# Keys and values of one pair of batches projected among the other pair's recurrences, and half of the routing in the last attention steps

## What is computed

```python
# conditioning: forward and backward recurrences of exp(k) and exp(k)*v, k = v = fside
num = nf + nb - ekv + euk * vf
den = df + db - ek + euk
x0  = sigmoid(r) * (num / maximum(den, 1e-8)) * (0.8 + 0.2 * tf)
# attention on the conditioned rows, 16 query heads, 4 key/value heads, head size 128
h = rmsnorm(x0, ln_w)
q, k, v = h @ wq, h @ wk, h @ wv ;  q, k = apply_rope(q), apply_rope(k)
attn = softmax(causal(q @ k.T / sqrt(128)))
x1 = (attn @ v) @ wo + x0
# routing: best 2 of 8 experts of every token
h2 = rmsnorm(x1, ff_ln_w);  logits = h2 @ gate_w;  top_k(logits, 2)
```

## Time and profile before

| | us |
|---|---|
| median of 3 runs (625.84 to 627.07) | 626.72 |
| the profiled execution | 625.02 |
| its span, first to last instruction | 623.2 |
| recurrences, to the last x0 | 0 to 73 |
| last batch's hidden rows and keep-clock | 73 to 81 |
| keys and values | 81 to 108 |
| attention, steps 0 to 37 | 108 to 300 |
| routing and ranking | 300 to 328 |
| experts and second layer | 328 to 623 |

### The profile page before, as it was taken

The page is one execution under the profiler, slowest core; times in us unless marked ns, Lnnn a source line. Parts: engine busy times, 40 slices in busy tenths (PEclk is TensorE's granted clock), DMA queues, the critical chain, the costliest instruction groups (busy, mean ns, idle before and its releaser), DMA issues.

```text
span 623.2 us, 10889 instructions
## 1 busy us (share of the span) xinstructions
PE 495.9 (80%) x3862; PEld 406.4 (65%) x3862; DVE 506.2 (81%) x981; ACT 361.1 (58%) x762; POOL 241.2 (39%) x204
## 2 busy tenths in 40 slices
PE   2011298599999999999748999999999999475774
PEld 1000143278888878888618999999999999332542
DVE  4999878688888888987354979989999899489993
ACT  3336235777787778876307457565555556356671
POOL 3244014744444445541436079642514420170011
PEclk9999999989999999999859999999999999888897
DMA  8300004050000000000149799889888753130001
GB/s 267 135 1 1 0 1 135 0 178 2 1 2 2 1 2 9 19 9 2 58 157 357 259 331 281 273 267 257 300 290 271 274 130 119 34 103 17 9 25 36
DMA packets 36530, 71.87 MB, mean 115 GB/s; under 512 B 5275, under 2 KB 21915, under 8 KB 36219
## 3 DMA queue, kind: packets, MB, share of 16 engines
q10 hardware_dynamic: 15280, 40.77, 19.6%
q1 hardware_dynamic: 18123, 22.26, 10.6%
q0 software_dynamic: 3072, 8.14, 5.2%
HBM read 66.03 MB, written 5.12 MB: 114 GB/s over the span
## 4 chain that ended last, share of the span: by engine, by line
PE 55%; DVE 27%; issue 7%; ACT 5%; DMA 3%; POOL 1%; SPq 1%; DVEq 0%; ACTq 0%; POOLq 0%; PEldq 0%
PE pw L437 9%; PE pb L437 9%; PE pt L631 6%; PE pb L631 6%; PE sc L478 6%; PE sc L631 6%; PE po L437 5%; PE pt L489 3%; DVE areg L1181 2%; DVE areg L1167 2%; DVE areg L1165 2%; DVE rs L1579 2%; DMA wreg<-in_L_ffn_w 1%; DVE breg L1238 1%; DVE areg L1614 1%
## 5 line engine op out<-in xcount | busy, mean ns | idle before, releaser
L1730 POOL TENSOR_TENSOR breg<-breg,con 128x512 f32<-128x512 f32 x32 | 40.7, 1272 | 81.4 <-ACT breg L864 81.4
L437 PE MATMUL pb<-areg,wreg 128*128 128x512 f16 x240 | 58.4, 379 | 2.1 <-ACT breg L864 1.9
L437 PE MATMUL pw<-areg 128*128 128x256 f16 x406 | 56.5, 273 | 2.7 <-DVE areg L1533 2.7
L872 ACT ACTIVATE breg<-breg,mx 128x128 f32<-128x128 f32 (+1 forms) x128 | 56.5, 444 | 2.0 <-DVE mx L1289 2.0
L478 PE MATMUL sc<-areg,breg 128*128 128x128 f32 (+1 forms) x256 | 48.6, 334 | 6.7 <-DVE mx L1289 5.5
L631 PE MATMUL pb<-areg,wreg 128*128 128x128 f32 x448 | 52.7, 275 | 0.6 <-ACT areg L965 0.6
L985 ACT CAST areg<-areg 128x512 f16<-128x512 f32 (+1 forms) x46 | 25.9, 563 | 46.8 <-DVE areg L1519 43.6
L631 PEld LDWEIGHTS pb<-areg,wreg 128*128 128x128 f32 x448 | 51.3, 192 | 0.9 <-issue 0.8
L631 PE MATMUL pt<-areg,wreg 128*128 128x128 f32 x424 | 49.9, 275 | 1.3 <-DMA wreg<-in_L_ffn_w 1.3
L631 PEld LDWEIGHTS pt<-areg,wreg 128*128 128x128 f32 x424 | 48.5, 192 | 1.5 <-DMA wreg<-in_L_ffn_w 1.4
L631 PE MATMUL sc<-areg,wreg 128*128 128x128 f32 x416 | 48.9, 275 | 0.0
(11 more groups left out here) (250 smaller groups left out, 1286.4 us busy)
## 6 DMA issues: line engine op xcount, KB each, us to landing
wreg<-in_L_ffn_w ACTq DMA_DIRECT2D x40, 896.0 KB, 8.1
wreg<-in_L_ffn_w SPq DMA_DIRECT2D x14, 896.0 KB, 8.3
ys_dram<-areg ACTq DMA_DIRECT2D x23, 128.0 KB
wreg<-in_L_ffn_wq SPq DMA_DIRECT2D x1, 2048.0 KB, 8.9
wreg<-in_L_ffn_wo SPq DMA_DIRECT2D x1, 2048.0 KB, 8.2
areg<-in_fside_BxSxS ACTq DMA_DIRECT2D x4, 256.0 KB, 5.4
x_in<-in_x SPq DMA_DIRECT2D x4, 256.0 KB, 3.9
h_dram<-areg SPq DMA_DIRECT2D x8, 128.0 KB, 1.7
```

What stands on the lines that cost most here:

```text
L437: last = nc.tensor.matmul(bank, w(a), m(b), start=first and k == 0, stop=final and k == 2)
L872: last = nc.scalar.activation(pr[:, parity, b, o:o + w], pr[:, parity, b, o:o + w], ACT.Exp, bias=mx[:, parity, k:k + 1], scale=-1.0, accu ...
L1730: G.tensor_tensor(t2[:, parity, :].rearrange("p (b n) -> p b n", b=2), t2[:, parity, :].rearrange("p (b n) -> p b n", b=2), rope_sin.rearr ...
```

## The change

Instructions are moved, hardly any are added. Six edits:

1. The recurrence loop on VectorE is unrolled. Batches 0 and 1 run as before. Then scans of batch 2, the low parts of the key and value weights, the low hidden rows of batches 0 and 1, and from there the `rope` products, sine products and low value parts of n = 0 to 3 stand between the parts of batches 2 and 3. ScalarE, GpSimd and TensorE follow the same order; TensorE's keep-clock stands after batch 1.
2. ScalarE splits the key and value weights after batch 0 and the query weights after batch 1 (`qkvhi_done` counts to 2). VectorE makes the low query parts at the end of batch 3.
3. n = 4 to 7 (pair 1) are projected in steps 1 to 4, in bank pb[1], with the sine product on GpSimd. `query_place` and `key_place` give the order of all 40 rotations: keys 0 to 3, queries 0 and 1, then key, query in turn. All queries use pb[0]. The low hidden rows of batches 2 and 3 are made in step 0.
4. The output weights are split in steps 5, 7, 9 and 11.
5. Four row tiles are transposed in steps 34 to 37 and three multiplied in 35 to 37; logits go to bank sc2; 10 keep-clock products stand ahead of tile 4 and 8 behind tile 7. Keep-clock of steps 1, 2 moves to 0, 1.
6. xn, the sigmoids and the squares' waste output live elsewhere, so that nothing overlaps.

```diff
+OUT_WEIGHTS_AT = (5, 7, 9, 11)
+        def query_place(u):
+            return KVH + u + max(0, u - 1) if u <= KVH else KU + u
+        def key_place(n):
+            return n if n < KVH else KVH + 2 + 2 * (n - KVH)
+        def route_bank(i):
+            return pb[i % 2] if i >= NT // 2 else pb[0]
...
-            for b in range(B):
+            for b in range(2):
                 ratio_transposes(b)
                 hidden_transposes(b)
...
-            pe.wait_ge(s["hlo_done"], B)
-            pe.wait_ge(s["hi_done"], B)
+            pe.wait_ge(s["hlo_done"], 2)
+            pe.wait_ge(s["hi_done"], 2)
...
-            for n in range(KU):
-                if n >= 2:
+            def key_bank(n):
+                return pb[n % 2] if n < KVH else pb[1]
+            def keys_and_values(n):
+                if n >= KVH:
+                    pe.wait_ge(s["swap_done"], key_place(n - 1) + 1)
+                elif n >= 2:
                     pe.wait_ge(s["swap_done"], n - 1)
...
+            keys_and_values(0)
+            ratio_transposes(2)
+            keys_and_values(1)
+            hidden_transposes(2)
+            keys_and_values(2)
+            keys_and_values(3)
+            ratio_transposes(3)
+            hidden_transposes(3)
...
             def step(u, parity):
                 if within(u, 0):
-                    pe.wait_ge(s["swap_done"], KU + u - 1 if u < LAG else KU + u)
-                    proj(None, query_bank(u), (u % H) * HD, u // H)
-                if u == 1:
-                    pe.wait_ge(s["vlo_done"], NT)
-                if u in (1, 2):
-                    keep_clock(pw[:, :], 4)
+                    pe.wait_ge(s["swap_done"], query_place(u - 1) + 1 if u >= 1 else key_place(2) + 1)
+                    proj(None, pb[0], (u % H) * HD, u // H)
+                if u in (0, 1):
+                    keep_clock(sc2[:, 1, :], 4)
...
+                if u == 5:
+                    pe.wait_ge(s["vlo_done"], NT)
+                    pe.wait_ge(s["swap_done"], key_place(KU - 1) + 1)
...
+                if u == 1:
+                    pe.wait_ge(s["hlo_done"], B)
+                    pe.wait_ge(s["hi_done"], B)
+                if 1 <= u <= KVH:
+                    keys_and_values(KVH + u - 1)
+                if u >= QU + 2:
+                    route_transposes(u - QU - 2)
+                if u >= QU + 3:
+                    route_products(u - QU - 3)
...
-            for i in range(NT + 1):
+            route_products(NT // 2 - 1)
+            keep_clock(pt2[:, 1, :], 10)
+            for i in range(NT // 2, NT + 1):
                 if i < NT:
                     route_transposes(i)
-                if i >= 1:
+                if i > NT // 2:
                     route_products(i - 1)
+            keep_clock(pt2[:, 1, :], 8)
...
+            squares(0)
+            normalise_rows(0)
+            exponential_of_keys(2, 0, cond_buf[0])
+            hidden_high(0)
+            split_keys_and_values()
+            exponential_of_sums(2, 0, cond_buf[0])
+            squares(1)
+            normalise_rows(1)
+            exponential_of_keys(3, 1, cond_buf[0])
+            hidden_high(1)
+            split_queries()
+            exponential_of_sums(3, 1, cond_buf[0])
+            swap_and_value(0)
+            squares(2)
+            swap_and_value(1)
+            normalise_rows(2)
+            swap_and_value(2)
+            hidden_high(2)
+            swap_and_value(3)
+            squares(3)
+            normalise_rows(3)
+            hidden_high(3)
...
+                if 1 <= u <= KVH:
+                    swap_and_value(KVH + u - 1)
+                if u in OUT_WEIGHTS_AT:
+                    wo_high(OUT_WEIGHTS_AT.index(u))
...
+                if u >= QU + 2:
+                    copy_h2T(u - QU - 2)
...
+            for i in range(NT // 2, NT):
+                squares_of_tile(i)
+            for i in range(NT // 2, NT):
                 copy_h2T(i)
...
+            scans(2, 0)
+            link(scans(2, 1))
+            dve.wait_ge(s["qkvhi_done"], 1)
+            for c in range(C):
+                for q in range(2):
+                    low_lanes(c, q, H, H + KVH)
...
+            hidden_low(0)
+            hidden_low(1)
+            add_terms(2)
+            invert(2)
+            dve.wait_ge(s["con_in"], 16)
+            rope(0, pb[0], 0)
+            mixing_ratio(2)
+            first_input(2)
+            scans(3, 0)
+            times_sin(0)
+            v_low(0)
+            rope(1, pb[1], 1)
+            link(scans(3, 1))
+            times_sin(1)
+            v_low(1)
+            rope(2, pb[0], 0)
+            add_terms(3)
+            times_sin(2)
+            v_low(2)
+            rope(3, pb[1], 1)
+            invert(3)
+            times_sin(3)
+            v_low(3)
+            mixing_ratio(3)
+            dve.wait_ge(s["qkvhi_done"], 2)
+            low_lanes(0, 0, 0, H)
+            first_input(3)
+            low_lanes(0, 1, 0, H)
+            low_lanes(1, 0, 0, H)
+            low_lanes(1, 1, 0, H).then_inc(s["qkvlo_done"], 1)
...
+                if u == 0:
+                    hidden_low(2)
+                    hidden_low(3)
+                if 1 <= u <= KVH:
+                    n = KVH + u - 1
+                    rope(key_place(n), pb[1], key_place(n) % 2)
+                    v_low(n)
+                if u in OUT_WEIGHTS_AT:
+                    wo_low(OUT_WEIGHTS_AT.index(u))
...
                 if within(u, 0):
-                    rope_sum(KU + u, parity)
+                    rope_sum(query_place(u), query_place(u) % 2, qr[:, parity, :], u)
+                if 1 <= u <= KVH:
+                    n = KVH + u - 1
+                    rope_sum(key_place(n), key_place(n) % 2, key_home(n))
```

178 lines of the change are left out of this document (81 added, 97 removed).

## The result

The changed kernel takes 623.39 us (median of 8 executions, 620.9 to 626.18) against 626.68 for the kernel before beside it: ratio 0.9946, 95% interval 0.9920 to 0.9972, so **3.3 us or 0.54% faster**. Executed again for a second profile it took 624.36 (12 executions, 621.79 to 625.60) against 626.87: ratio 0.9960 (0.9944 to 0.9976), 2.5 us. The forecast was 620.8, range 616.3 to 624.8.

What follows compares the result with a forecast made beforehand. Bound by VectorE's recurrences and the serial work after them, then by TensorE, full from 140 us. 4.2 us won ahead of unit 7 plus 1.7 at the end make 5.9: median 626.72 to 620.8, range 616.3 to 624.8.

Steps and rivals of the forecast that it cites:

- Recurrences: Batches 2 and 3 on VectorE, interleaved with keys and values 0 to 3: x0 of batch 3 done at 88.2 us.
- the two meetings: GpSimd's bonus product and key sum lengthen VectorE instructions among the recurrences: 0.9 each, 1.8 us, bounded by 0 and 4.
- From x0 to step 0: After x0 at 88.2, three low query parts run under ScalarE's squares and GpSimd's root; TensorE's transposes end at 92.6.
- Steps 1 to 4: Attention steps projecting keys and values 4 to 7: 4.9, 5.3, 5.2 and 6.8 us, the four engines nearly even.
- the rival on the other side: TensorE's clock falls in steps 1 to 4: one slow step leaves 625.8 us, two make 631; chance 0.07.
- Steps 5 and 6: Step 5 begins at 119.4, its VectorE work ends at 130.4; step 6 ends with unit 7 projected at 133.7, before deductions.
- The fall of the clock that I had struck out: The kernel before's clock drop at 124 to 126 us (0.67 granted) was taken as gone in the new steps.
- Sum at unit 7: Unit 7 projected 6.5 us earlier than 140.20, less 1.8 and 0.5 for VectorE-GpSimd meetings: 4.2 us won.
- Output weights in steps 5 to 11: Splitting them on VectorE and ScalarE costs nothing; 1.6 us if the cover is gone.
- The end: Routing partly moved into steps 34 to 37, clock held for tile 7: 1.7 us won, bounded by 0.3 and 2.5.
- All behind 328 moves as one: From 328 us, the experts, to the end everything shifts together, so the 5.9 us won ahead reaches the end.

Runs made afterwards that it cites:

- the low parts drawn ahead: Changed kernel with the four low query parts on VectorE moved earlier, into its waits around batches 2 and 3: 623.73 us, ratio 0.9946.
- old routing: Changed kernel with the routing of the kernel before, all eight row tiles routed after the last step: 623.32 us, ratio 0.9941.
- the routing alone: Kernel before with only the new routing edit added, its attention otherwise as before: 626.25 us, ratio 0.9985.

## Why the prediction was nearly right, and where it was not

- **Recurrences.** Forecast was the end of x0 of batch 3 at 88.2, or 90.0 with the two meetings; it starts at 87.8 to 88.5 and takes 0.69, so it ends at 88.5 to 89.2. The price of 2.6 for six products at the lower level was right (2.77 at 72.83), and so, nearly, was VectorE's wait of 3.0 (2.55; in the second profile these six took 2.12 and the wait was 1.49). The low key parts were not held by GpSimd's TENSOR_SCALARs, as forecast: four in 1.52 us at 50.01, beside GpSimd's two from 49.53 to 52.46. The meetings came where they were put, at the bonus product and the key sum:

```profile
49.53 2.93 POOL L295 TENSOR_SCALAR areg<-ratio,wu 128x256 f32<-128x256 f32 x2
50.01 1.52 DVE L1285 SCALAR_TENSOR_TENSOR wreg<-wreg 128x256 f16<-128x256 f32 x4
...
54.19 1.26 POOL L1811 TENSOR_TENSOR areg<-areg,ratio 128x512 f32<-128x512 f32 x1 [1.73 <-ACT areg L832]
54.36 2.30 DVE L1223 SCALAR_TENSOR_TENSOR areg<-areg,decay 128x510 f32<-128x510 f32 x2
...
85.45 1.26 POOL L1816 TENSOR_TENSOR areg<-breg 128x512 f32<-128x512 f32 x1 [4.48 <-DVE breg L1303]
85.89 1.37 DVE L1259 SCALAR_TENSOR_TENSOR areg<-areg,tf 128x512 f32<-128x512 f32 x1
```

  2.30 instead of the 1.41 of the earlier trace rows, and 1.37 for one that takes 0.74 elsewhere in the trace: 0.9 and 0.6. They are there, 1.5 where 1.8 was forecast, and the stretch still ends 0.8 to 1.5 ahead of 90.0, so the order laid out by hand was 0.5 to 1.2 too long elsewhere.
- **From x0 to step 0.** Here a step failed. "Three more low query parts run under ScalarE's squares, GpSimd's root" counted only VectorE as the one that is held. It works the other way as well: GpSimd's root took 2.84 instead of 0.89, and from x0's end to the end of the transposes it was 6.1 (89.23 to 95.30) and not 4.4; with the low parts drawn ahead it was 4.1 (89.55 to 93.67). With the meetings in both, that end is 0.9 late against the forecast (94.4). I had read from L1155 beside GpSimd's TENSOR_SCALAR that such a pair doesn't meet. The Trainium skill, page "SBUF — State Buffer", section "SBUF: two separate sides", says that whichever of the two starts first keeps the shared port for its whole instruction, and the other stands. At 90.26 the trace agrees: 1.28 us for two columns, which ends about when the second of the three low parts does. At 49.79 of the trace of before, and at 50.01 here, it does not. What tells the two places apart no run here shows.
- **Steps 1 to 4.** The forecast times were 4.9, 5.3, 5.2 and 6.8; the projections of queries 1 to 5 at 99.85, 104.61, 109.8, 115.0 and 121.99 give 4.76, 5.19, 5.20 and 6.99. GpSimd, not VectorE, is what the chain goes through there (108.62 above). The clock stayed up, so the rival on the other side did not come.
- **Steps 5 and 6.** "The new steps leave no wait of TensorE over 1.5 us" was wrong: 1.74 at 129.41, behind 1.08. The fall of the clock that I had struck out came back in three of eight profiles, at 1.5 us each.
- **Sum at unit 7.** 4.2 forecast, 3.06 in the first profile. Over all profiles of this code, old routing among them, unit 7's cosine product stands at 137.33 on average and at 141.41 in the three with the attention of before: 4.1; its projection on TensorE moved by 4.3. Step 5 stood at 121.99 where 121.7 was forecast, and from there to unit 7's projection it was 15.0 where the clock fell and 13.4 where the wait was filled (121.85 to 135.27), against 14.3 forecast. So the sum is right by luck in part: the recurrences ended 0.8 to 1.5 early and the root was 1.7 late, and the 14.3 for steps 5 and 6 lie between what they take with the fall of the clock and without it.
- **Output weights in steps 5 to 11.** Costed at nothing. TensorE's projection of the unit at 274.38 before came at 271.48 after, 2.90 of the 3.06 kept: 0.16.
- **The end.** Transposes in the last steps cost 0.5 and not 1.15, and net 1.2 to 1.5 were won instead of 1.7, of which the routing, exchanged inside the changed kernel, accounts for 0.8. Residual and logits of the first profile:

```profile
298.04 0.69 DVE L1397 SCALAR_TENSOR_TENSOR x<-pb,x 128x512 f32<-128x512 f32 x1 [1.98 <-PEq L573]
...
305.20 0.22 DVE L1443 COPY rt<-sc 128x64 f32<-128x64 f32 x1 [1.83 <-PE sc L552]
```

  7.16 from one to the other; before, 8.68 (300.49 to 309.17).
- **All behind 328 moves as one.** This is the step that failed by most. 5.9 were forecast at the experts' start and 5.4 came; of these 2.5 to 3.3 reached the end. The median lies inside the range, though little more than half of the forecast gain came. Places where it can be given back were found at three points that the earlier trace rows showed as one row with a clock of 0.96: the last down products (1.2 to 2.2 more where the clock fell in a wait that was always there), ScalarE's issue of the last up weights (about 2.0 where it was long), and the second layer's first row tile (1.3 where the clock fell, 0.4 to 0.7 where it did not). The first two account for the whole of the stretch from the second expert tile to the first gather, in all 14 profiles. With all three covered or moved the changed kernel stands 5.1 under the kernel before with two of them covered, by medians that are each uncertain by over 1.

What stays open: whether these three hit the changed kernel more often, and if so why. Where they were not covered, the last down products were slow in five of eight profiles with the changed attention and in one of two with that of before (3.64 us in the routing alone), the second layer's up products in two of six and none of two, and ScalarE's issue was long in five of ten and none of three. That is too few to tell. The medians point that way (1.1 to 2.0 from covering two waits in the changed kernel, 0.6 in the kernel before) but don't settle it. That an earlier start meets the chip at another moment is a guess and not shown. Nor is it shown what ScalarE's issue waited for.

## What to carry to other kernels

A wait of TensorE is not only its own length: price the products behind it at the lower level too, in every stage, also in those that the change only shifts, and fill such waits with products of zeros before judging a change of 0.5%. Compare several profiles by marks inside them: one pair gave equal spans for a gain of 3.3 us. Work moved under another engine's idle time can lengthen what little that engine still has to do there: two tiny GpSimd instructions on the path took 2.84 instead of 0.89 us. Two edits that each fill the same idle time don't add: look at which instruction ends last after the first one.

## What the runs showed of the hardware

- The same wait (1.74 us ahead of unit 6, 2.71 ahead of the last down products) brought TensorE's clock down in some executions and left it up in others: 2.74 or 1.47 us for six products, 3.93 or 2.47 for the 21 of the last down products. The Trainium skill, page "TensorE: Matmul & The Clock Gate", section "What's actually happening", says that the number of slow products at a kernel's start varies from run to run; these rows show the like in the middle of a kernel.
- 102 products of zeros among the recurrences made the kernel 6 us faster: transposes 0.66 instead of 1.12, six products 1.46 instead of 2.77. Step 0 came 3.0 to 4.1 earlier with them on the same engine.
- A GpSimd instruction on two columns took 1.28 instead of 0.19 us beside VectorE's product of two on-chip operands of 1024 columns. The other way round, VectorE's instructions on two on-chip operands were not held by GpSimd's TENSOR_SCALARs (1.52 for four of 256 columns), but were by its TENSOR_TENSOR (2.30 instead of 1.41).
- ScalarE's issue of one pair of loads took 0.91 in some executions and 3.4 to 4.7 in others at the same place of the program, with ScalarE standing meanwhile; the load given to SyncE was issued in 0.90.
